# A decoder layer on one core: the batch loop's long calls are cut into parts and four engine programs get a new order inside a step

## The reference

```python
x = x + self_attention(norm(x))   # 16 heads of 8; scores * tril(-1), then softmax; output @ Wr + br
x = x + cross_attention(norm(x))  # one head of 128, over 1601 context rows of the sequence
x = x + ffn(norm(x))              # 8 experts, top 2 of a softmax gate, and one shared expert
```

## Time and profile before

| | |
|---|---|
| median of 3 runs | 706.94 us (706.55 to 707.15) |
| the profiled execution | 704.75 us |
| its span, first to last instruction | 702.9 us |
| busy PE, DVE, ACT, POOL | 630.3, 434.9, 474.8, 467.7 us |

### The profile page before, as it was taken

How to read it: one execution, slowest core, us unless ns; L and a number is a source line. 1 busy time by engine, 2 the same in 40 slices (tenths; PEclk the granted TensorE clock), 3 DMA queues, 4 the chain that set the end, 5 groups by cost and what they waited for, 6 DMA issues and landing times.

```text
span 702.9 us, 17394 instructions
## 1 busy us (share of the span) xinstructions
PE 630.3 (90%) x5381; PEld 486.7 (69%) x5426; DVE 434.9 (62%) x1476; ACT 474.8 (68%) x1106; POOL 467.7 (67%) x784
## 2 busy tenths in 40 slices
PE   5877799998999999999999999898999579999994
PEld 2343468676677776777677676677878468888883
DVE  2356566877777777876868777774555533333337
ACT  3334677877878787787877878678776246666650
POOL 4335466677878787796877878758656416666665
PEclk9759999999999999999999999999999899999998
DMA  4923435452452525434353453502222423333129
GB/s 143 232 52 83 129 95 160 102 159 46 154 148 69 171 51 159 115 96 145 84 159 77 124 153 71 167 20 93 94 63 59 90 68 100 103 87 86 50 72 308
DMA packets 65114, 77.98 MB, mean 111 GB/s; under 512 B 9314, under 2 KB 50679, under 8 KB 64896
## 3 DMA queue, kind: packets, MB, share of 16 engines
q1 hardware_dynamic: 59884, 67.70, 34.8%
q0 software_dynamic: 4352, 8.47, 4.0%
q10 hardware_dynamic: 788, 0.69, 0.4%
HBM read 54.30 MB, written 22.64 MB: 109 GB/s over the span
## 4 chain that ended last, share of the span: by engine, by line
POOL 32%; PE 32%; issue 18%; DMA 6%; DVE 4%; ACT 3%; SPq 2%; another core or an unknown queue 2%; POOLq 0%; DVEq 0%; ACTq 0%
POOL prob L2237 7%; PE banks L337 7%; POOL sorted_rows L2262 5%; PE banks L359 4%; PE banks L1088 3%; POOL rstd L2148 3%; POOL info_lo L2226 3%; PE banks L1050 3%; PE banks L348 2%; POOL parts L2177 2%; POOL qk_r L2175 2%; PE banks L1070 2%; PE banks L825 2%; DMA qst<-q_parts 2%
## 5 line engine op out<-in xcount | busy, mean ns | idle before, releaser
L1503 ACT ACTIVATE prob<-banks 128x512 f32<-128x512 f32 x192 | 114.6, 601 | 54.0 <-PE banks L828 52.0
L2237 POOL TENSOR_SCALAR_AFFINE_SELECT prob<-prob 128x256 f32<-128x256 f32 (+1 forms) x192 | 91.8, 500 | 56.4 <-ACT prob L1503 56.1
L1088 PE MATMUL banks<-info,xprobT 128*128 128x128 f32 (+1 forms) x832 | 104.0, 276 | 1.2 <-issue 1.0
L1088 PEld LDWEIGHTS banks<-info,xprobT 128*128 128x128 f32 (+1 forms) x832 | 100.4, 192 | 3.1 <-issue 1.5
L1779 DVE CUSTOM_DVE_ANT_0 masked<-banks,mask 128x256 f32<-128x256 f32 x208 | 78.4, 414 | 14.9 <-PE banks L823 13.2
L2262 POOL DMA_INDIRECT sorted_rows<-row,place x64 | 64.3, 1005 | 23.7 <-issue 18.2
L1819 DVE TENSOR_REDUCE xmax<-banks 128x1 f32<-128x896 f32 x64 | 63.0, 985 | 27.3 <-PE banks L1050 20.1
L1784 DVE TENSOR_REDUCE mx<-banks 128x4 f32<-128x512 f32 x64 | 44.2, 690 | 56.6 <-remote 50.9
L828 PE MATMUL banks<-qst,kst 51*128 51x128 bf16 (+1 forms) x512 | 75.0, 249 | 0.1
L1070 PE MATMUL banks<-cst,xprob 128*128 128x128 f32 (+1 forms) x416 | 70.6, 283 | 0.6 <-ACT xprobT L1373 0.2
L1373 ACT COPY xprobT<-banks 128x512 f32<-128x512 f32 (+2 forms) x128 | 64.8, 506 | 8.5 <-PE banks L1070 7.5
(11 more groups left out here) (206 smaller groups left out, 1645.9 us busy)
## 6 DMA issues: line engine op xcount, KB each, us to landing
infoT<-in_ctxT SPq DMA_DIRECT2D x16, 800.5 KB, 5.5
info<-in_ctx SPq DMA_DIRECT2D x16, 448.0 KB, 3.8
kst<-k_stack SPq DMA_DIRECT2D x31, 192.0 KB
info<-in_ctx SPq DMA_DIRECT2D x16, 320.0 KB
q_parts<-parts SPq DMA_DIRECT2D x31, 96.0 KB, 2.3
k_stack<-parts SPq DMA_DIRECT2D x31, 96.0 KB, 2.3
qst<-q_parts SPq DMA_DIRECT2D x31, 96.0 KB
infoT<-sorted_rows SPq DMA_DIRECT2D x36, 65.0 KB, 1.9
```

What stands on the lines that cost most here:

```text
L1088: mm = pe.matmul(ps[:, V_BANK, u * P:(u + 1) * P], lhsT=xprobT[hf][0:w, m - blocks[0], :], rhs=info[0:w, m, :], start=(m == blocks[0]), st ...
L1503: act.activation(prob[n % 2][:, kind * 512:(kind + 1) * 512], ps[:, gamma_bank_of(b, v), :], ACT.Exp, scale=SCALE).then_inc(s["p_exp"], 1)
L2237: pool.affine_select(out=w, in_=w, compare_op=ALU.is_gt, fill=0.0, base=0, pattern=[[0, 4 if kind == 2 else 2], [1, P]], channel_multiplie ...
```

## The change

Long calls take one more argument, the part to run: `cross_scores` and `cross_values` on PE two parts, `normalised1/2/3` and `gate_exp` on ACT two, `statistics1/2/3` and `cross_add` two, `negative_maxima` and `places` five and `choices` nine on DVE, `inverse_deviation` three, `masked_sums` and `cross_den` two on POOL. The parts together issue what the whole call issued; each keeps the waits of its own instructions. In `begin()` and `finish()` the parts of a call follow one another, so their order is that of before. In `step(i)` the parts of PE, ACT, DVE and POOL are placed in a new order. SP's program is the same instruction for instruction. Some calls pass from one step's list to the next one's: POOL's `masked(i, 8..10)` and ACT's `cross_copy(k, 1, 0)` change the step in which they stand (and so have a copy in `begin()` or `finish()`), and DVE's `statistics1(f + 2)` stands at the head of a step and not at the end of the one before.

```diff
-            def cross_scores(k, u):
+            def cross_scores(k, u, z):
...
-                pieces = ((0, 512), (512, H0)) if hf == 0 else ((H0, H0 + 512),)
-                for c, (m0, m1) in enumerate(pieces):
+                if z == 0 or hf == 0:
+                    m0, m1 = ((0, 512), (512, H0))[z] if hf == 0 else (H0, H0 + 512)
                     for n, (a, b) in enumerate(((q2_hi, info_hi), (q2_hi, info_lo), (q2_lo, info_hi))):
...
             def step(i):      # TensorE
-                cross_values(l, 3)
+                cross_values(l, 3, 0)
+                cross_values(l, 3, 1)
                 out_T(j, 0)
+                scores(i, 0)
                 cross_transposes(k, 0, 0)
-                scores(i, 0)
-                cross_scores(k, 1)
+                cross_scores(k, 1, 0)
                 out_T(j, 1)
+                cross_scores(k, 1, 1)
                 scores(i, 1)
...
             def step(i):      # ScalarE
+                info_high(j, 0)
                 on_T(j)
                 p_exp(g, 4)
+                if i > STEPS[0]:
+                    cross_copy(k, 1, 0)
                 cross_exp(k, 2)
                 p_exp(g, 5)
                 cross_copy(k, 1, 1)
                 query_key(f)
+                p_exp(g, 6)
                 split_cast(f, 0)
-                p_exp(g, 6)
-                info_high(j, 0)
...
             def step(i):      # GpSimd
-                masked(g, 8)
-                masked(g, 9)
-                masked(g, 10)
                 masked(g, 11)
                 cross_weight(k)
+                masked_sums(i, 0)
+                info_low(j, 1)
+                residual(g)
+                deviation1(f + 2, 0)
                 row_inputs(l)
-                info_low(j, 1)
                 masked(i, 0)
-                masked_sums(i)
...
```

More of the change, by code:

```diff
@@ L1953, in step @@
+                choices(l, 2)
+                choices(l, 3)
                 alpha_max(i, 10)
+                choices(l, 4)
+                choices(l, 5)
                 query_low(j)
+                heads_out(g, 0)
                 alpha_max(i, 11)
-                negative_maxima(i)
-                places(l)
                 cross_rec(k)
+                negative_maxima(i, 0)
+                choices(l, 6)
+                negative_maxima(i, 1)
+                places(l, 0)
+                negative_maxima(i, 2)
@@ L1959, in step @@
+                negative_maxima(i, 3)
+                places(l, 1)
+                negative_maxima(i, 4)
                 cross_max(j, 0)
                 heads_out(g, 1)
-                cross_add(k)
+                cross_add(k, 0)
+                choices(l, 7)
+                places(l, 2)
+                cross_add(k, 1)
+                places(l, 3)
                 head_sums(g, 0)
                 alpha_max(f, 0)
-                statistics3(k)
+                statistics3(k, 0)
                 head_sums(g, 1)
+                statistics3(k, 1)
@@ L1966, in step @@
                 cross_max(j, 1)
-                head_rec(g)
                 alpha_max(f, 1)
                 value_heads(f)
+                head_rec(g)
                 alpha_max(f, 2)
+                choices(l, 8)
+                places(l, 4)
                 alpha_max(f, 3)
@@ L2064, in finish @@
                 gate_shift(B - 4)
-                choices(B - 4)
+                choices(B - 4, 0)
+                choices(B - 4, 1)
+                choices(B - 4, 2)
+                choices(B - 4, 3)
+                choices(B - 4, 4)
+                choices(B - 4, 5)
+                choices(B - 4, 6)
+                choices(B - 4, 7)
+                choices(B - 4, 8)
                 cross_rec(B - 3)
@@ L2087, in finish @@
                 cross_max(B - 1, 0)
-                cross_add(B - 2)
-                statistics3(B - 2)
+                cross_add(B - 2, 0)
+                cross_add(B - 2, 1)
+                statistics3(B - 2, 0)
+                statistics3(B - 2, 1)
                 cross_max(B - 1, 1)
-                choices(B - 3)
-                places(B - 3)
+                choices(B - 3, 0)
+                choices(B - 3, 1)
+                choices(B - 3, 2)
+                choices(B - 3, 3)
+                choices(B - 3, 4)
+                choices(B - 3, 5)
+                choices(B - 3, 6)
+                choices(B - 3, 7)
+                choices(B - 3, 8)
+                places(B - 3, 0)
+                places(B - 3, 1)
+                places(B - 3, 2)
+                places(B - 3, 3)
+                places(B - 3, 4)
                 cross_max(B - 1, 2)
@@ L2096, in finish @@
                 gate_shift(B - 2)
-                choices(B - 2)
+                choices(B - 2, 0)
+                choices(B - 2, 1)
+                choices(B - 2, 2)
+                choices(B - 2, 3)
+                choices(B - 2, 4)
+                choices(B - 2, 5)
+                choices(B - 2, 6)
+                choices(B - 2, 7)
+                choices(B - 2, 8)
                 cross_rec(B - 1)
                 hidden(1, 0)
-                cross_add(B - 1)
-                statistics3(B - 1)
+                cross_add(B - 1, 0)
+                cross_add(B - 1, 1)
+                statistics3(B - 1, 0)
+                statistics3(B - 1, 1)
                 hidden(1, 1)
-                places(B - 2)
+                places(B - 2, 0)
+                places(B - 2, 1)
+                places(B - 2, 2)
+                places(B - 2, 3)
+                places(B - 2, 4)
                 add_shared(0)
@@ L2107, in finish @@
                 add_shared(1)
-                choices(B - 1)
-                hidden(2, 1)
-                places(B - 1)
+                choices(B - 1, 0)
+                choices(B - 1, 1)
+                choices(B - 1, 2)
+                choices(B - 1, 3)
+                choices(B - 1, 4)
+                choices(B - 1, 5)
+                choices(B - 1, 6)
+                choices(B - 1, 7)
+                choices(B - 1, 8)
+                hidden(2, 1)
+                places(B - 1, 0)
+                places(B - 1, 1)
+                places(B - 1, 2)
+                places(B - 1, 3)
+                places(B - 1, 4)
                 slots()
@@ L2369, in begin @@
                 masked(2, 6)
-                cross_den(0)
+                cross_den(0, 0)
+                cross_den(0, 1)
                 masked(2, 7)
+                masked(2, 8)
+                masked(2, 9)
+                masked(2, 10)
             def finish():
```

639 lines of the change are left out of this document (397 added, 242 removed).

## The result

The changed kernel took 726.78 us (median of 4 runs, 723.37 to 729.70) against 706.89 us of the kernel before on the same chip: a ratio of 1.028, interval 1.0232 to 1.0328. It is slower by 19.9 us; I had forecast 700.4 us, 6.5 us faster. The profiled execution took 723.37 us (span 721.5) against 704.75 (702.9), 18.6 us more.

What follows compares the result with a forecast made beforehand. A ring was taken to bound each loop step: a 3.2 us trip plus 26.7 us, the latter falling to 26.2. Thirteen steps of 29.4 instead of 29.9 us save 6.5: 706.94 to 700.4 us, range 697 to 704 (8 in 10: 692.5 to 711).

Steps and rivals of the forecast that it cites:

- The bound: In the loop, PE is nearly dense, but a ring, not the sum of its matmuls, closes each 29.90 us step.
- the trip: From the maxima's transposition to the next step's first scores: 3.2 us, fixed by ACT, SP and a DMA, not shortened.
- The waits that should go: PE's waits before scores 5, scores 8, cross scores (`q2_lo`) and a small rest before scores 6: gain 1.2 us a step.
- The cuts: Four PE calls cut with another group between the halves, adding group boundaries: +0.05 us a step, bounds 0 and +0.4.
- ACT: New waits, chiefly scores 6 and 7 for ACT between exponentials 4 and 6: +0.2 us a step, bounds 0 and +1.2.
- the fifth: POOL beside DVE's `choices` in the loop: contention slows POOL by 0.45 us a step, within its slack, costed at nothing.
- its slack: POOL's spare time from the trip's start to `cross_den` and the maxima: 1.5 us a step, 1.0 after contention with DVE.
- the sum: Per loop step: 26.7 - 1.2 + 0.44 + 0.05 + 0.2 = 26.2, plus 3.2: 29.4 us against 29.9.
- The rival on the slower side: ACT sets the scores in mid-step, new waits reach 1.2 us: 30.4 us a step, 713.4 us; chance 0.20.
- handed back: Transposes' 0.44 and 0.3 to 0.7 us of new waits eat the 1.2: 29.8 a step, 705.6 us; chance 0.24.

Runs made afterwards that it cites:

- mended_vb: Changed kernel with info_low, split_rest, cross_transposes(k, 0, 0) and values(g, 0) at old places, dummy matmuls before two stack loads: 710.51 us, 1.0061 of the kernel before.
- mended_ct_d: Changed kernel with info_low, split_rest and cross_transposes(k, 0, 0) at old places, dummy matmuls before two stack loads: 708.74 us, 1.0071 of the kernel before.
- before_low_late_d: Kernel before with POOL's info_low(g, 0) moved behind deviation1(f + 2), beside DVE's choices: 715.30 us, ratio 1.0144; on the slower kind of chip 747.80 us, 1.0174.
- awake: Changed kernel with dummy matmuls on PE, 14 ahead of scores(3, 0) and 7 ahead of scores(15, 6): 784.52 us, 1.0664 of the kernel before, slower kind of chip.
- mended: Changed kernel with info_low and split_rest at old places, 11 and 7 dummy matmuls before two stack loads: 782.19 us, 1.0683 of the kernel before, slower chip.
- low_early: Changed kernel with POOL's info_low(g, 0) and split_rest(f + 1, 1) at old places: ratios to the kernel before 1.0611, 1.0599 and 1.0681 on slower chips, 1.0180 on a faster.
- control in set 5: The changed kernel itself run again beside its variants, on a chip where the kernel before took 705.07 us: 725.44 us, ratio 1.0281.

## Why the prediction was wrong

**The bound and the trip** were right for the inner steps. The trip is as long as before and PE idles 0.8 us a step ahead of scores 0; I had 0.9. Moving `cross_transposes(k, 0, 0)` costs about what I put on it, 0.44: taking it back gave 0.3 a step, with no other edit in the inner steps. The 2.0 us that I quoted from the Trainium skill (DMA: Bandwidth & Descriptors, Anatomy of one DMA) is given there for GpSimd's DMA path, while this transfer is SP's; as the trip did not change, no run here tests it.

**The waits that should go** went. (In my count 1.12 - 0.44 - 0.1 is 0.58, not 0.55, which changes nothing.) `q_lo` and scores 5 have no wait in the list of after; `xrec` still costs POOL 0.7 a step of the 1.6 of before, not nothing; the wait ahead of `emc` is 2.5, forecast 2.4.

**The cuts and ACT** can't be priced one by one, but PE waits for no exponential in the eight steps, where I had 0.2. Without the hold, 1.5 us, the step would be 29.45 us by subtraction, my 29.4; that is an estimate, and no run showed such a step: with the hold gone a step took 30.1 on the A chip, and the best that ran there 29.7 (`mended_vb`) and 29.8 (`mended_ct_d`), both with the transposes back. So the gain of 1.2 us, from the waits that went, was never seen in a time.

**The failed step is the fifth, contention between DVE and POOL.** I looked for it at the right place (`choices` beside the split and `info_low`) and named the loser wrongly. From a POOL operation of 0.72 and 0.82 us I worked out 0.45 us a step lost by POOL and hidden in its slack. What happens is that DVE's instruction loses all that is left of POOL's, 1.9 us at a time, and on DVE a maximum is queued behind it. I costed `choices` on DVE at its old durations. Size: +1.5 us of PE idle time a step, where I had 0. The inner steps came out 1.0 us longer where the sum has them 0.5 shorter, which puts the eleven of them 16.8 us off the sum. The step after that was missing as well: `choices` parts 1 to 3 stand ahead of `alpha_max(i, 10)`, and I had weighed only maximum 9 behind part 0.

The Trainium skill has the rule in full on another page than the one I used (SBUF — State Buffer, Who interferes with whom): a VectorE instruction with two SBUF inputs and a GpSimd one that reads SBUF exclude each other for a whole instruction, and the later to issue is blocked until the first ends. The trace agrees where the order can be read: in `before_low_late_d` `info_low` starts 0.22 us ahead of `above` and `above` takes 2.06 us beside its 2.14, and in step 4 of the changed kernel it starts 0.25 us ahead of `biased`, which takes 1.86 us. By that rule the price would have been the rest of `info_low`, about 2 us on DVE by its 2.11 us in the kernel before (an estimate), in place of 0.45 on POOL.

**The outer steps** were missed too. I multiplied one step by thirteen. Steps 3 and 15 have no full set of calls, PE waits longer for a stack load, and the clock fell behind the longer wait: +4.4 and +5.0 us where the sum has -0.5 each. In step 15 1.1 is the hold, 0.7 the longer wait and 2.8 the clock; in step 3 0.9 is the later load, 1.6 the clock and 1.0 a wait for ACT's `xn1T`, while some 0.9 stays unexplained. I had costed the stack loads at 0 to 0.3 in some steps. For the clock in step 3 there are also the dummies (2.1 to 3.2 us back in `awake`, `mended` and `mended_ct_d` against `low_early` of the same set); for step 15 there is one pair of profiles of the same kernel.

**The rival** on the slower side had the right sign and a wrong mechanism: ACT sets no scores in the inner steps. And some 0.6 of the 1.45 us that the hold's removal should return was taken on the A chip by `xdiff`, which is my rival "handed back" at work.

## What to carry to other kernels

Before moving an operation on VectorE or GpSimd, list the VectorE instructions that read two tensors in SBUF, and lay the long GpSimd ones (one SBUF input was enough here) beside the new places: a VectorE instruction of 0.2 us costs what is left of its neighbour, and so does all that is queued behind it. Look at the longest of a group in the trace, not at its mean. Price the first and last steps of a loop on their own, and treat a wait of TensorE like the 1.67 us of step 15 as one that may cost its clock too.

## What the runs showed of the hardware

- The hold also comes from masks, which have one tensor input: `above` 0.82 us instead of 0.29 beside one. A copy on VectorE that turns float32 into int32 is held as well (`place`, 0.38 instead of 0.16 us, ending 0.02 us after the mask). Of the instructions that read PSUM and one SBUF tensor `masked` is not: it takes 0.39 to 0.43 us in all 208 records of the changed kernel, 47 of which began beside a POOL instruction with more left to run.
- The granted clock was half after waits for a stack load of 1.67, 1.81, 3.06 and 3.20 us and was not after such waits of 0.95, 1.68 and 2.01 us, so the length alone doesn't decide. The hold's own waits of 1.67 us ahead of scores 11 went both ways too (step 5 of the changed kernel: 1.00; of its control in set 5: half).
- Chips differ. The same kernel took 705 to 707 or 730 to 734 us, and a change that costs 2.8% on one kind costs 6.8% on the other, where TensorE's results are seen 2.2 us late in each step with indirect DMAs and the clock falls behind that. With the old order (`before_low_late`) the delay stood in one step alone. What causes it is open.
